# Values multiplied in pairs of key tiles, with three steps of probabilities kept, in an attention and state-space kernel

## The chip, the cores and the metric

The kernel runs on one core of one Trainium2 chip. The metric is the device time of one execution, in microseconds (us); several executions are timed and the median is given. One more execution is recorded by the profiler, and all rows below are of that one.

## The reference, cut to what matters

Two residual blocks follow each other. The first is attention with styles, for a batch of 8, a sequence of 1024, a width of 512 and 16 heads of 32:

```python
x = x + attention(x, cond, ...)     # the block that the change touches
x = x + scan_block(x, cond, ...)    # a gated state-space scan, untouched

# in attention, for every batch and head (x is styled and normalised before)
q, k, v = heads(x @ Wq.T * q_dc), heads(x @ Wk.T * k_dc), heads(x @ Wv.T * v_dc * s2)
attn = softmax(q @ k.T * scale)
out = attn @ v
out = out @ Ww.T * w_dc + skip @ Wu.T * u_dc
```

All inputs, probabilities and values are fp32.

## The kernel before, in words

One program runs two stages in turn: attention, then the scan. Attention works in 32 units, a unit being one batch with a group of 4 heads (`GH`), and in each unit in 16 steps: 2 query chunks of 512 columns (`c`), and in each of them 8 key tiles of 128 keys (`kt`, `TT` = 8). A step `n` has these pieces for its key tile:

- `S`: four score matmuls, one a head, each into a PSUM bank of its own (L802).
- `E`: four exponentials on ScalarE (L948), from the banks into SBUF. For `kt` = 0 they go into `acc` (two chunks deep), for the others into `prob`, which has two slots; step `n` writes slot `n % 2`.
- `C`: the values. Four narrow matmuls, 128 keys by 32 columns of V each, the four heads side by side in the four groups of 32 columns of TensorE's array (L815), added up in one PSUM bank over the 8 key tiles of the chunk. fp32 makes two instructions of each matmul, so the rows show 8 for a piece.
- `A`: for `kt` = 1 to 6, GpSimd adds the four tiles of `prob` to `acc` (L1126), so as to have the sum over keys. The first of them changes `acc`, which `C` of `kt` = 0 reads, so it waits for that `C`.

After a chunk comes `N`: eight narrow matmuls with ones, four over `prob` of `kt` = 7 (L827) and four over `acc` (L831), which give the softmax sums; the latter wait for the last `A`. Then ScalarE copies the sums out (L954), VectorE inverts them (L1074) and multiplies the values (L1084).

Other work, the side work, shares the engines: for the next unit the projections of queries and keys (`pm`, L773) and a pass over all scores to find their maxima (`mx`, L785, reduced by VectorE at L1055), and for the batch the values (L726), the skip path (L744, transposes at L736), the output (L754), the normalisation (L1109 on GpSimd) and the scaling of weights (L1115 on GpSimd).

The order of the instructions on each engine is fixed when the program is built, by a planner (`Order`, L105): each lane is a list of pieces with an assumed cost, what they come after and which bank they take, and the planner always places the piece that can start first by its own clock, and of pieces that can start together the one that is due first. Pieces of one lane and one engine keep their order. The main lane is what `attend` lists (L365 to L408). On TensorE it reads: S(0), S(1), C(0), S(2), C(1), and so on; C(7) and then N come behind the S of the next chunk's first step. `S` takes one of banks 0 to 3, side work takes one of banks 2 to 5, the values lie in bank 6 or 7. Side work may not be placed before its due step. On the chip each engine executes its list in order and waits on semaphores.

The exponential of step `n` writes a slot of `prob` when its last user is done: `C` and `A` of step `n - 2`, or, where step `n - 2` was the last of a chunk (`kt` = 7), `C` and `N` of it (L934 to L947).

Of the kernel before, what the change touches and what calls it, by code (L numbers as in the profile page):

```python
# [16 lines left out]
P = 128  # L17
HID = 512
HEADS = 16
DH = HID // HEADS  # L20
GH = P // DH
# [5 lines left out]
NX = 3 * NST  # L27
EPS_LN = 1e-5
EPS_DEMOD = 1e-8
BANK = 512  # L30
TAPS = 4
UNIT = 8
# [187 lines left out]
    return h, qc * (TT // NQ) + t, qc, kc  # L220


def attention_plan(plan, B, TT, NQ):
    plan.bank = {}
    order = Order(plan, 8, (0.2, 0.2))
# [139 lines left out]
    def attend(u):  # L365
        out, put_ = lane()
        b, g = divmod(u, GROUPS)

        def put(t, *a, **k):
            put_(*a, **k)  # L370
            out[-1]["due"] = u * n_steps + t - 1.0
        for n in range(n_steps + 3):
            if n < n_steps:
                c, kt = divmod(n, TT)

                if kt == 0:
                    v = u * NQ + c - 2
                    old = lambda h: (("N", v // NQ, v % NQ),) if v >= 0 else ()
                else:
                    v = u * n_steps + n - 2  # L380
                    v -= 2 if v % TT == 0 else 0
                    last = ("N", v // n_steps, v % n_steps // TT) if v % TT == TT - 1 else None
                    old = lambda h: (("C", v // n_steps, v % n_steps), last or ("A", v // n_steps, v % n_steps, h)) if v >= 0 else ()
                for h in range(GH):
                    s = ("S", u, n, h)
                    put(n, "PE", 0.24, s, (("mst", u),) if n == 0 else (), [("pe_m{m}", 1)], take=EXP, group=s,
                        step=u * n_steps + n)
                    put(n, "ACT", 0.6, ("E", u, n, h), (s,) + old(h), [("act_m{m}", 1)], group=s, give=True)
            if 0 < n <= n_steps:
                k = n - 1  # L390
                c, kt = divmod(k, TT)
                put(n - 0.5, "PE", 1.0, ("C", u, k), tuple(("E", u, k, h) for h in range(GH)) + (("mv_o", b, TT - 1),),
                    [("pe_av", 1)], take=(6 + (u * NQ + c) % 2,) if kt == 0 else None, group=("av", u, c))
                if 0 < kt < TT - 1:
                    for h in range(GH):
                        put(n - 0.5, "POOL", 1.28, ("A", u, k, h), (("E", u, k, h),) + (
                            (("C", u, k - 1),) if kt == 1 else (("A", u, k - 1, h),)), [("pool_acc", 1)])
            if n and n % TT == 0:
                c = n // TT - 1
                g = ("N", u, c)  # L400
                put(n, "PE", 1.95, g, tuple(("A", u, c * TT + TT - 2, h) for h in range(GH)), [("pe_m{m}", 1)], take=SIDE, group=g)
                put(n, "ACT", 0.6, ("R", u, c), (g,) + ((("D", u - (c == 0), (c - 1) % NQ),) if u or c else ()),
                    [("act_m{m}", 1)], group=g, give=True)
                put(n, "DVE", 3.4, ("I", u, c), (("R", u, c),), [("dve_norm", 1)])
                put(n, "DVE", 0.7, ("D", u, c), (("I", u, c), ("C", u, c * TT + TT - 1)) + (
                    (("f_mm", b - 1, (c + 1) * TT // NQ - 1, HT - 1),) if b else ()), [("dve_norm", 1)], group=("av", u, c), give=True)
        return out
# [34 lines left out]
class Attention:  # L442
    def __init__(self, nc, ctx, d, ident, ones32, B, S):
# [36 lines left out]
        setup.close()  # L480
        self.qhat = sb("qhat", [P, 2, GH, S], F32R)
        self.khat = sb("khat", [P, 2, GH, S], F32R)
        self.prob = sb("prob", [P, 2 * GH, QC])

        self.aoT = sb("aoT", [P, GROUPS, S])

# [218 lines left out]
    def tensor(self, pe):  # L705
# [4 lines left out]
        for p in plan.pieces:  # L710
# [66 lines left out]
            elif kind == "mx":  # L777
                u, j = at
                m = plan.bank[p]
                h, qt, qc, c = score_tile(j, TT, self.NQ)  # L780
                s = u % 2
                for k in (2 * qc, 2 * c + 1):
                    self.half_laid(w, u, k)
                self.empty(w, m, p)
                pe.matmul(bank[m][:, 0:QC], self.qhat[0:96, s, h, qt * P:(qt + 1) * P],  # L785
                          self.khat[0:96, s, h, c * QC:(c + 1) * QC], start=True, stop=True).then_inc(sem[f"pe_m{m}"], 1)
            elif kind == "mt":
                u, = at
                m = plan.bank[p]
                w.wait_ge(sem["dve_mx"], plan.after("dve_mx", ("mxr", u)))  # L790
                self.empty(w, m, p)
                pe.transpose(bank[m][0:GH * TT, 0:P], self.mx[:, :], ident[:, :]).then_inc(sem[f"pe_m{m}"], 1)
            elif kind == "S":
                u, n, h = at
                m = plan.bank[p]
                c, kt, a = self.step(u, n)
                s = u % 2
                w.wait_ge(sem["kones"], 2)
                self.laid(w, u)
                w.wait_ge(sem[f"ld_mrow{s}"], plan.after(f"ld_mrow{s}", ("mst", u)))  # L800
                self.empty(w, m, p)
                pe.matmul(bank[m][:, 0:QC], self.khat[0:98, s, h, kt * P:(kt + 1) * P],  # L802
                          self.qhat[0:98, s, h, c * QC:(c + 1) * QC], start=True, stop=True).then_inc(sem[f"pe_m{m}"], 1)
            elif kind == "C":
                u, n = at
                c, kt, a = self.step(u, n)
                b, g = divmod(u, GROUPS)
                w.wait_ge(sem["dve_v"], plan.after("dve_v", ("mv_o", b, TT - 1)))
                if u * self.NQ + c > 1:

                    w.wait_ge(sem["dve_norm"], plan.after("dve_norm", ("D", *divmod(u * self.NQ + c - 2, self.NQ))))
                for h in range(GH):
                    self.of_bank(w, "act", ("S", u, n, h), ("E", u, n, h))
                    of = self.acc[:, a, h, :] if kt == 0 else self.prob[:, (n % 2) * GH + h, :]
                    mm = pe.matmul(bank[6 + a][h * DH:(h + 1) * DH, 0:QC], self.value(b, kt, g)[:, h * DH:(h + 1) * DH],  # L815
                                   of, start=kt == 0, stop=kt == TT - 1)
                mm.then_inc(sem["pe_av"], 1)
            elif kind == "N":
                u, c = at
                m = plan.bank[p]  # L820
                a = (u * self.NQ + c) % 2
                self.empty(w, m, p)

                n = c * TT + TT - 1
                for h in range(GH):
                    self.of_bank(w, "act", ("S", u, n, h), ("E", u, n, h))
                    pe.matmul(bank[m][h * DH:(h + 1) * DH, 0:QC], self.ones32[:, :], self.prob[:, (n % 2) * GH + h, :],  # L827
                              start=True, stop=False)
                for h in range(GH):
                    w.wait_ge(sem["pool_acc"], plan.after("pool_acc", ("A", u, n - 1, h)))  # L830
                    mm = pe.matmul(bank[m][h * DH:(h + 1) * DH, 0:QC], self.ones32[:, :], self.acc[:, a, h, :],  # L831
                                   start=False, stop=True)
                mm.then_inc(sem[f"pe_m{m}"], 1)
# [22 lines left out]
    def scalar(self, act):  # L856
        sem, plan, w, TT, QC, bank = self.sem, self.plan, Waits(act), self.TT, self.QC, self.bank
        w.wait_ge(sem["x_dve"], 2 * TT + 3)
        for p in plan.pieces:
# [65 lines left out]
            elif kind == "E":  # L925
# [8 lines left out]
                        self.of_bank(w, "pe", old, old)  # L934
                    to = self.acc[:, a, h, :]
                else:
                    v = u * self.NQ * TT + n - 2
                    v -= 2 if v % TT == 0 else 0
                    if v >= 0:
                        old = divmod(v, self.NQ * TT)  # L940
                        w.wait_ge(sem["pe_av"], plan.after("pe_av", ("C", *old)))
                        if v % TT == TT - 1:
                            sums = ("N", old[0], old[1] // TT)
                            self.of_bank(w, "pe", sums, sums)
                        else:
                            w.wait_ge(sem["pool_acc"], plan.after("pool_acc", ("A", *old, h)))
                    to = self.prob[:, (n % 2) * GH + h, :]  # L947
                act.activation(to, bank[m][:, 0:QC], ACT.Exp, scale=SCALE).then_inc(sem[f"act_m{m}"], 1)  # L948
            elif kind == "R":
                u, c = at  # L950
# [145 lines left out]
    def gpsimd(self, pool):  # L1096
# [5 lines left out]
        for p in plan.pieces:  # L1102
# [14 lines left out]
            elif kind == "A":  # L1117
# [1 line left out]
                c, kt, a = self.step(u, n)  # L1119
                self.of_bank(w, "act", ("S", u, n, h), ("E", u, n, h))  # L1120
                if kt == 1:
                    w.wait_ge(sem["pe_av"], plan.after("pe_av", ("C", u, n - 1)))
                    self.of_bank(w, "act", ("S", u, n - 1, h), ("E", u, n - 1, h))
                else:
                    w.wait_ge(sem["pool_acc"], plan.after("pool_acc", ("A", u, n - 1, h)))
                pool.tensor_tensor(self.acc[:, a, h, :], self.acc[:, a, h, :], self.prob[:, (n % 2) * GH + h, :],  # L1126
                                   ALU.add).then_inc(sem["pool_acc"], 1)


# [1245 lines left out]
```

## Time and profile before

| | |
|---|---|
| median of 3 runs | 6185.2 us (6185.17 to 6187.26) |
| profiled execution | 6190.7 us, span 6188.9 us |
| TensorE busy | 5830.7 us, 94% of the span |
| VectorE, ScalarE, GpSimd busy | 72%, 39%, 52% |
| attention | about the first 3150 us of the span |

Busy times are of instructions as the profiler records them; a matmul's recorded time is longer than the distance to the next one, since matmuls are pipelined, so TensorE's busy share says little, and the distances between starts say more. PE is TensorE's matmuls, PEld its weight loads, DVE VectorE, ACT ScalarE, POOL GpSimd.

### The profile page before, as it was taken

How to read it: one execution, taken by the hardware profiler on the slowest of the kernel's cores; microseconds unless marked ns; L12 is line 12 of the kernel's file. 1: busy time of each engine (PE TensorE's matmuls, PEld its weight loads, DVE VectorE, ACT ScalarE, POOL GpSimd, SP SyncE). 2: the span in 40 equal slices, each digit the busy share in tenths (PEclk: the TensorE clock that was granted, in tenths of full speed). 3: DMA queues.
4: the chain of work that ended last, by engine and by line, in shares of the span. 5: the costliest groups of instructions: out<-in, count | busy, mean ns of one | idle time of the engine just before them, and what ended most of it. 6: DMA issues, size and time to landing. Idle time of an engine off the chain costs nothing. (4 is left out here: it accounts for less than half of the span.)

```text
span 6188.9 us, 73250 instructions
## 1 busy us (share of the span) xinstructions
PE 5830.7 (94%) x24000; PEld 2703.2 (44%) x24000; DVE 4474.3 (72%) x5676; ACT 2407.5 (39%) x4698; POOL 3217.6 (52%) x2625
## 2 busy tenths in 40 slices
PE   7999999999999999999986879999999999999998
PEld 3444444444444444444443424444443444444343
DVE  4656656556556566565546998999999898999983
ACT  2444444445444454444453424243332423334111
POOL 1876767677667776775743323425243443524213
PEclk7999999999999999999988889999999999999999
DMA  2332323333232332323213343534444443544433
GB/s 86 89 91 69 99 73 94 91 88 89 76 96 77 98 93 69 106 60 96 82 67 109 87 113 103 147 96 131 110 116 126 121 133 89 150 96 128 115 91 115
DMA packets 411565, 613.30 MB, mean 99 GB/s; under 512 B 58768, under 2 KB 189968, under 8 KB 410672
## 3 DMA queue, kind: packets, MB, share of 16 engines
q1 hardware_dynamic: 374320, 558.24, 32.4%
q10 hardware_dynamic: 36864, 50.38, 3.2%
q8 instruction: 190, 3.11, 0.2%
q14 instruction: 191, 1.56, 0.1%
HBM read 305.31 MB, written 201.38 MB: 82 GB/s over the span
## 5 line engine op out<-in xcount | busy, mean ns | idle before, releaser
L1126 POOL TENSOR_TENSOR acc<-acc,prob 128x512 f32<-128x512 f32 x1536 | 1906.4, 1277 | 837.3 <-PE bank L815 570.8
L1055 DVE TENSOR_REDUCE mx<-bank 128x1 f32<-128x512 f32 x2048 | 1307.4, 684 | 535.9 <-PE bank L785 529.6
L2091 DVE SCALAR_TENSOR_TENSOR g<-xps,bd,g 128x1024 f32<-128x1024 f32 x1024 | 1313.2, 1282 | 143.8 <-PE xps L1806 68.1
L1806 PE MATMUL xps<-sx,spread 128*128 128x512 f32 x2048 | 910.4, 529 | 140.6 <-DVE g L2091 126.0
L948 ACT ACTIVATE prob<-misc 128x512 f32<-128x512 f32 x1277 | 713.5, 599 | 739.0 <-PE misc L802 653.6
L785 PE MATMUL bank<-khat,qhat 96*128 96x512 f32 x2048 | 939.1, 519 | 5.9 <-DVE mx L1055 0.9
L2097 DVE TENSOR_SCALAR g<-g,lim 128x1024 f32<-128x1024 f32 x1024 | 892.7, 872 | 34.8
L1806 PEld LDWEIGHTS xps<-sx,spread 128*128 128x128 f32 x2048 | 359.0, 195 | 693.8 <-issue 368.0
L802 PE MATMUL misc<-qhat,khat 98*128 98x512 f32 x1443 | 602.6, 460 | 17.8 <-ACT prob L948 11.7
L785 PEld LDWEIGHTS bank<-khat,qhat 96*128 96x128 f32 x2048 | 373.8, 192 | 532.5 <-issue 381.4
L1820 PE MATMUL yps<-g,cexp 128*32 128x512 f32 x4096 | 585.4, 630 | 0.1
L773 PE MATMUL bank<-xhT,wqk 128*128 128x512 f32 x1024 | 490.7, 606 | 2.6 <-ACT rsum L954 1.7
L815 PE MATMUL bank<-prob,V 128*32 128x512 f32 x3584 | 489.4, 616 | 0.0
L1763 PE MATMUL miscb<-x2T_sb,w_in 128*128 128x512 f32 x952 | 473.5, 607 | 8.1 <-DMA x2T_sb<-scratch_x2T 8.1
L1860 PE MATMUL miscb<-w_out,ygT 128*128 128x512 f32 x944 | 467.9, 605 | 1.7 <-ACT ygT L2031 1.3
L2231 POOL TENSOR_TENSOR cexp<-cd,mask 128x256 f32<-128x256 f32 x128 | 78.8, 616 | 721.3 <-DVE g L2097 463.0
L1830 PE MATMUL miscb<-w_in,x2T_t 128*128 128x512 f32 x896 | 434.1, 604 | 2.5 <-DMA x2T_t<-scratch_x2T 2.4
L802 PEld LDWEIGHTS misc<-qhat,khat 98*128 98x128 f32 x1443 | 270.6, 190 | 253.4 <-issue 115.0
L2270 POOL TENSOR_TENSOR y_t<-y_t,dx_t 128x512 f32<-128x512 f32 x118 | 150.5, 1276 | 441.9 <-DVE g L2097 333.0
L1046 DVE SCALAR_TENSOR_TENSOR halves<-bank,qk_dc,halves 128x512 fp32r<-128x512 f32 x128 | 95.2, 744 | 372.7 <-ACT halves L912 372.6
L1074 DVE RECIPROCAL rsum<-rsum 128x512 f32<-128x512 f32 x64 | 214.3, 3349 | 190.5 <-ACT rsum L954 190.5
L1910 ACT ACTIVATE xr<-miscb,temb 128x128 f32<-128x128 f32 x476 | 135.6, 368 | 555.5 <-PE miscb L1763 555.5
(221 smaller groups left out, 7189.6 us busy)
## 6 DMA issues: line engine op xcount, KB each, us to landing
sx<-scratch_xhl SPq DMA_DIRECT2D x512, 128.0 KB, 4.9
scratch_dx<-dx SPq DMA_DIRECT2D x64, 512.0 KB, 3.2
scratch_xhl<-xhi SPq DMA_DIRECT2D x64, 512.0 KB, 4.9
scratch_xhl<-xn SPq DMA_DIRECT2D x64, 512.0 KB, 5.1
scratch_y<-ysb SPq DMA_DIRECT2D x512, 64.0 KB
dx_t<-scratch_dx SPq DMA_DIRECT2D x59, 512.0 KB, 6.1
y_t<-scratch_y SPq DMA_DIRECT2D x59, 512.0 KB, 3.9
xt_n<-in_x SPq DMA_DIRECT2D x112, 256.0 KB, 3.0
```

The lines of the kernel that those rows point to most:

```text
L773: mm = pe.matmul(bank[m][:, 0:QC], self.wqk[:, n, it, :], self.xhT[:, it, c * QC:(c + 1) * QC], start=it == 0, stop=it == HT - 1)
L785: pe.matmul(bank[m][:, 0:QC], self.qhat[0:96, s, h, qt * P:(qt + 1) * P], self.khat[0:96, s, h, c * QC:(c + 1) * QC], start=True, stop=Tru ...
L802: pe.matmul(bank[m][:, 0:QC], self.khat[0:98, s, h, kt * P:(kt + 1) * P], self.qhat[0:98, s, h, c * QC:(c + 1) * QC], start=True, stop=Tru ...
L815: mm = pe.matmul(bank[6 + a][h * DH:(h + 1) * DH, 0:QC], self.value(b, kt, g)[:, h * DH:(h + 1) * DH], of, start=kt == 0, stop=kt == TT - 1)
L948: act.activation(to, bank[m][:, 0:QC], ACT.Exp, scale=SCALE).then_inc(sem[f"act_m{m}"], 1)
L1055: dve.tensor_reduce(self.mx2[:, h * TT + qt, c:c + 1], bank[m][:, 0:QC], AX.X, ALU.max).then_inc(sem[f"dve_m{m}"], 1)
L1126: pool.tensor_tensor(self.acc[:, a, h, :], self.acc[:, a, h, :], self.prob[:, (n % 2) * GH + h, :], ALU.add).then_inc(sem["pool_acc"], 1)
L1763: mm = pe.matmul(bank[m][:, :], self.w_in[:, it, ct * P:(ct + 1) * P], self.x2T[:, it, :, :].rearrange("p b q -> p (b q)"), start=it == 0, ...
L1806: mm = pe.matmul(self.xps[t % 2][:, half * BANK:(half + 1) * BANK], self.spread[:, 2 * part + half, :], self.sx[:, n % 2, wd, :], start=Tr ...
L1820: mm = pe.matmul(bank[2 + m][32 * j:32 * (j + 1), :], self.cexp[:, h, tc, :], self.g[:, (t + tp) % 4, half * BANK:(half + 1) * BANK], star ...
L2091: dve.scalar_tensor_tensor(self.g[:, t % 4, :], self.xps[t % 2][:, :], self.bd[:, i % 2, tl:tl + 1], self.g[:, (t - 1) % 4, :], ALU.mult, ...
L2097: dve.tensor_scalar(self.g[:, t % 4, :], self.g[:, t % 4, :], self.lim[:, i % 2, 0, tl:tl + 1], self.lim[:, i % 2, 1, tl:tl + 1], ALU.min, ...
```

## The change

`C` is made once for two key tiles, at each odd `kt`: eight narrow matmuls (16 instructions), first the four of the even tile and then the four of the odd one, each four with a semaphore increment of their own. On TensorE's list it reads: S(0), S(1), S(2), C(0, 1), S(3), S(4), C(2, 3), and so on, with C(6, 7) and N behind the S of the next chunk's first step. The planner is told 1.9 for the piece in place of 1.0 for each half. `prob` has three slots, filled in turn by the steps with `kt` > 0 alone (`ring`), so an exponential waits for the user of three such steps ago; the first `A` of a chunk waits for the first half of C(0, 1). `prob` grows from 16 to 24 KB a partition, and the memory set aside for descriptors of dynamic DMAs falls from 2048 to 512 bytes.

```diff
+PROBS = 3
+def ring(u, n, TT, NQ):
+    c, kt = divmod(n, TT)
+    return ((u * NQ + c) * (TT - 1) + kt - 1)
+def ring_user(r, TT, NQ):
+    c, kt = divmod(r, TT - 1)
+    return c // NQ, c % NQ * TT + kt + 1
...
-                    v = u * n_steps + n - 2
-                    v -= 2 if v % TT == 0 else 0
-                    last = ("N", v // n_steps, v % n_steps // TT) if v % TT == TT - 1 else None
-                    old = lambda h: (("C", v // n_steps, v % n_steps), last or ("A", v // n_steps, v % n_steps, h)) if v >= 0 else ()
+                    r = ring(u, n, TT, NQ) - PROBS
+                    uu, nn = ring_user(r, TT, NQ)
+                    last = ("N", uu, nn // TT) if nn % TT == TT - 1 else None
+                    old = lambda h: (("C", uu, nn | 1), last or ("A", uu, nn, h)) if r >= 0 else ()
...
-                put(n - 0.5, "PE", 1.0, ("C", u, k), tuple(("E", u, k, h) for h in range(GH)) + (("mv_o", b, TT - 1),),
-                    [("pe_av", 1)], take=(6 + (u * NQ + c) % 2,) if kt == 0 else None, group=("av", u, c))
+                if kt % 2:
+                    put(n - 0.5, "PE", 1.9, ("C", u, k), tuple(("E", u, j, h) for j in (k - 1, k) for h in range(GH)) + (
+                        ("mv_o", b, TT - 1),), [("pe_av", 2)], take=(6 + (u * NQ + c) % 2,) if kt == 1 else None,
+                        group=("av", u, c))
                 if 0 < kt < TT - 1:
                     for h in range(GH):
                         put(n - 0.5, "POOL", 1.28, ("A", u, k, h), (("E", u, k, h),) + (
-                            (("C", u, k - 1),) if kt == 1 else (("A", u, k - 1, h),)), [("pool_acc", 1)])
+                            (("C", u, k),) if kt == 1 else (("A", u, k - 1, h),)), [("pool_acc", 1)])
...
-        self.prob = sb("prob", [P, 2 * GH, QC])
+        self.prob = sb("prob", [P, PROBS * GH, QC])
...
-                for h in range(GH):
-                    self.of_bank(w, "act", ("S", u, n, h), ("E", u, n, h))
-                    of = self.acc[:, a, h, :] if kt == 0 else self.prob[:, (n % 2) * GH + h, :]
-                    mm = pe.matmul(bank[6 + a][h * DH:(h + 1) * DH, 0:QC], self.value(b, kt, g)[:, h * DH:(h + 1) * DH],
-                                   of, start=kt == 0, stop=kt == TT - 1)
-                mm.then_inc(sem["pe_av"], 1)
+                for n in (last - 1, last):
+                    kt = n % TT
+                    for h in range(GH):
+                        self.of_bank(w, "act", ("S", u, n, h), ("E", u, n, h))
+                        of = self.acc[:, a, h, :] if kt == 0 else self.prob[:, ring(u, n, TT, self.NQ) % PROBS * GH + h, :]
+                        mm = pe.matmul(bank[6 + a][h * DH:(h + 1) * DH, 0:QC], self.value(b, kt, g)[:, h * DH:(h + 1) * DH],
+                                       of, start=kt == 0, stop=kt == TT - 1)
+                    mm.then_inc(sem["pe_av"], 1)
...
-    nc = bacc.Bacc("TRN2", target_bir_lowering=False, num_devices=1, dynamic_dma_scratch_size=2048)
+    nc = bacc.Bacc("TRN2", target_bir_lowering=False, num_devices=1, dynamic_dma_scratch_size=512)
```

The reads of `prob` in `N` and `A` and the waits of `E` and `A` follow the same new numbering.

## Rows read from the trace of the kernel before

**Rows 1.** The page: busy time and share of each engine

```profile
PE 5830.7 (94%) x24000; PEld 2703.2 (44%) x24000; DVE 4474.3 (72%) x5676; ACT 2407.5 (39%) x4698; POOL 3217.6 (52%) x2625
```

**Rows 2.** Busy time by stretch: start:end, length, busy of each engine, clock, DMA

```profile
1500.00:2000.00 500.00, 486.05 (x2076) 230.57 (x2069) 301.13 (x452) 227.18 (x421) 348.58 (x282) 0.99 0.29 84
3050.00:3100.00 50.00, 43.14 (x183) 15.01 (x184) 11.21 (x15) 25.99 (x49) 40.97 (x34) 0.81 0.30 103
```

**Rows 3.** TensorE's groups by line, from 200 to 3100 us

```profile
L802 PE MATMUL misc<-qhat,khat 98*128 98x512 f32 x1405 | 585.0, 459 | 12.6 <-ACT prob L948 10.1 <-DMA qhat<-mrow 1.6
...
L815 PE MATMUL bank<-prob,V 128*32 128x512 f32 x3472 | 469.4, 612 | 0.0
...
L815 PE MATMUL bank<-acc,V 128*32 128x512 f32 x496 | 66.1, 605 | 0.0
```

**Rows 4.** TensorE in order of time, last unit: start, length, instructions

```profile
3071.17 0.39 PE L802 MATMUL bank<-qhat,khat 98*128 98x512 f32 x1
3071.40 0.39 PE L802 MATMUL misc<-qhat,khat 98*128 98x512 f32 x1
3071.63 0.40 PE L802 MATMUL bank<-qhat,khat 98*128 98x512 f32 x1
3071.96 1.07 PE L815 MATMUL bank<-prob,V 128*32 128x512 f32 x8
3072.95 0.50 PE L802 MATMUL misc<-qhat,khat 98*128 98x512 f32 x1
```

**Rows 5.** TensorE in order of time, narrow pieces back to back

```profile
603.16 2.19 PE L815 MATMUL bank<-prob,V 128*32 128x512 f32 x16
605.28 3.70 PE L773 MATMUL bank<-xhT,wqk 128*128 128x512 f32 x8
...
660.92 1.06 PE L815 MATMUL bank<-prob,V 128*32 128x512 f32 x8
661.80 1.04 PE L827 MATMUL bank<-prob,ones 128*32 128x512 f32 x8
662.66 1.04 PE L831 MATMUL bank<-acc,ones 128*32 128x512 f32 x8
663.63 0.50 PE L785 MATMUL bank<-khat,qhat 96*128 96x512 f32 x1
```

**Rows 6.** What TensorE's matmuls waited for, 200 to 3100 us

```profile
PE bank L792 <- DVE mx L1063: 41.6, 31, 1.9
PE misc L802 <- ACT prob L948: 10.1, 22, 1.2
PE bank L802 <- ACT rsum L954: 9.3, 20, 3.0
```

**Rows 7.** Who waited for the adds of GpSimd (L1126), 200 to 3100 us

```profile
  ACT prob L948: 47.6, 37
  PEld bank L831: 3.3, 4
```

**Rows 8.** GpSimd's groups by line, 200 to 3100 us

```profile
L1126 POOL TENSOR_TENSOR acc<-acc,prob 128x512 f32<-128x512 f32 x1488 | 1847.0, 1277 | 729.3 <-PE bank L815 566.9 <-ACT prob L948 127.3 <-issue 35.1
L1109 POOL TENSOR_TENSOR xt_n<-xt_n,brow 128x512 f32<-128x512 f32 x109 | 139.0, 1278 | 83.8 <-DMA xt_n<-in_x 82.9 <-ACT prob L948 0.7
L1115 POOL TENSOR_TENSOR wwu<-wwu,brow 128x512 f32<-128x512 f32 x62 | 79.7, 1285 | 31.9 <-DMA wwu<-in_wwT 31.9
```

**Rows 9.** GpSimd in order of time, at the ends of chunks

```profile
654.48 3.77 POOL L1126 TENSOR_TENSOR acc<-acc,prob 128x512 f32<-128x512 f32 x3
...
669.46 9.95 POOL L1126 TENSOR_TENSOR acc<-acc,prob 128x512 f32<-128x512 f32 x8 [5.88 <-PE bank L815]
...
884.81 5.00 POOL L1126 TENSOR_TENSOR acc<-acc,prob 128x512 f32<-128x512 f32 x4
906.21 4.96 POOL L1126 TENSOR_TENSOR acc<-acc,prob 128x512 f32<-128x512 f32 x4 [16.40 <-PE bank L815]
...
3104.53 6.24 POOL L1126 TENSOR_TENSOR acc<-acc,prob 128x512 f32<-128x512 f32 x5 [3.90 <-PE bank L815]
```

**Rows 10.** TensorE in order of time, the sums that wait for them

```profile
897.20 1.04 PE L831 MATMUL bank<-acc,ones 128*32 128x512 f32 x8
...
904.97 1.06 PE L815 MATMUL bank<-acc,V 128*32 128x512 f32 x8
```

**Rows 11.** The page: VectorE's maxima, the group by line

```profile
L1055 DVE TENSOR_REDUCE mx<-bank 128x1 f32<-128x512 f32 x2048 | 1307.4, 684 | 535.9 <-PE bank L785 529.6
```

**Rows 12.** The page: DMA issues, with the queue that issues them

```profile
sx<-scratch_xhl SPq DMA_DIRECT2D x512, 128.0 KB, 4.9
scratch_dx<-dx SPq DMA_DIRECT2D x64, 512.0 KB, 3.2
...
xt_n<-in_x SPq DMA_DIRECT2D x112, 256.0 KB, 3.0
```

More of the change, by code:

```diff
@@ L804, in tensor @@
             elif kind == "C":
-                u, n = at
-                c, kt, a = self.step(u, n)
+                u, last = at
+                c, _, a = self.step(u, last)
                 b, g = divmod(u, GROUPS)
@@ L826, in tensor @@
                     self.of_bank(w, "act", ("S", u, n, h), ("E", u, n, h))
-                    pe.matmul(bank[m][h * DH:(h + 1) * DH, 0:QC], self.ones32[:, :], self.prob[:, (n % 2) * GH + h, :],
+                    pe.matmul(bank[m][h * DH:(h + 1) * DH, 0:QC], self.ones32[:, :], self.prob[:, ring(u, n, TT, self.NQ) % PROBS * GH + h, :],
                               start=True, stop=False)
@@ L936, in scalar @@
                 else:
[L937 to L942, printed above, removed]
+                    r = ring(u, n, TT, self.NQ) - PROBS
+                    if r >= 0:
+                        old = ring_user(r, TT, self.NQ)
+                        w.wait_ge(sem["pe_av"], plan.after("pe_av", ("C", old[0], old[1] | 1)) - (1 - old[1] % 2))
+                        if old[1] % TT == TT - 1:
                             sums = ("N", old[0], old[1] // TT)
@@ L946, in scalar @@
                             w.wait_ge(sem["pool_acc"], plan.after("pool_acc", ("A", *old, h)))
-                    to = self.prob[:, (n % 2) * GH + h, :]
+                    to = self.prob[:, ring(u, n, TT, self.NQ) % PROBS * GH + h, :]
                 act.activation(to, bank[m][:, 0:QC], ACT.Exp, scale=SCALE).then_inc(sem[f"act_m{m}"], 1)
@@ L1121, in gpsimd @@
                 if kt == 1:
-                    w.wait_ge(sem["pe_av"], plan.after("pe_av", ("C", u, n - 1)))
+                    w.wait_ge(sem["pe_av"], plan.after("pe_av", ("C", u, n)) - 1)
                     self.of_bank(w, "act", ("S", u, n - 1, h), ("E", u, n - 1, h))
@@ L1125, in gpsimd @@
                     w.wait_ge(sem["pool_acc"], plan.after("pool_acc", ("A", u, n - 1, h)))
-                pool.tensor_tensor(self.acc[:, a, h, :], self.acc[:, a, h, :], self.prob[:, (n % 2) * GH + h, :],
+                pool.tensor_tensor(self.acc[:, a, h, :], self.acc[:, a, h, :], self.prob[:, ring(u, n, TT, self.NQ) % PROBS * GH + h, :],
                                    ALU.add).then_inc(sem["pool_acc"], 1)
```

## The prediction, made before the changed kernel was run

> **What bounds the kernel now.** I read the page first: TensorE is busy 94% of the span, the next engine 72% [rows 1]. The stretches come next, since the change touches attention alone, roughly the first 3150 of 6189 us. In the middle of it, from 1500 to 2000 us, TensorE is busy 486 of 500 us at a clock of 0.99, which is the level of 2.4 GHz, VectorE 301, ScalarE 227 and GpSimd 349 [rows 2]. The waits say the same: of 2900 us TensorE's matmuls waited 42 us for the maxima at the unit's end and some 20 us for banks that ScalarE had to empty [rows 6]. So attention goes by what TensorE has to execute, in a fixed order, and a piece made cheaper there is worth its own size, unless a new wait takes it back.
>
> The candidate for such a wait is GpSimd. The reader should see three numbers. A chunk lasts 2900 us / (496 / 8) = 46.8 us, since 496 rows are the eight instructions of C(0) of each chunk [rows 3], so a step lasts 5.85 us. The 24 adds of a chunk take 24 x 1.277 = 30.7 us, and with the 171 side pieces, 3.5 us a chunk, GpSimd is busy for 34 of 46.8 us [rows 8]. The adds run back to back from kt = 1 on, and the idle time lies in front of the first of them, which waits for C(0): 567 us in all [rows 8].
>
> **What a piece of C costs.** The order in time of the last unit shows it free of other work: scores start 0.23 us apart (3071.17, 3071.40, 3071.63), the piece of C starts 0.33 us behind the last score, and the next score 0.99 us behind the piece [rows 4]. Where narrow pieces stand together, the distances are 0.88, 0.86 and then 0.97 us [rows 5]. Eight more narrow instructions cost 0.86 to 0.88 us, then, and what is left of a lone piece is the price of going from wide to narrow (0.33 - 0.23 = 0.10 us) and back (0.99 - 0.86 = 0.13 us): 0.23 us.
>
> **What is removed.** 32 units of 16 steps have 512 pieces of C; the stretch of 2900 us holds (3472 + 496) / 8 = 496 of them [rows 3]. Half of them, 256, join another and lose 0.23 us each: 59 us. Two pieces of C already stand together in 8 places of the stretch, like the one of 603.16 [rows 5], where nothing is to be saved on that score, so I take 57 us. C(7) next to N stays what it was. The number of instructions, their data and the semaphore increments are the same.
>
> The bound from the other side is the row at 603.16: two pieces in 2.12 us [rows 5], which is 2.12 + 0.10 = 2.22 us against 2 x 1.09 = 2.18 us for two lone ones, no saving at all. Something inside that pair waited; the second piece needs exponentials of its own step, which had just been scored. In the changed order four scores of the next step stand between a step's last score and its C, nearly everywhere, and the even half of the pair is a whole step old, so I go by the clean rows: 0.23 us; the range keeps nothing as the other end.
>
> For the same switch the Trainium skill ("TensorEngine Tiling (Array Packing)", Key Properties) says that a change of tiling mode drains the engine; it gives no figure. The page "TensorE: Matmul & The Clock Gate" (Part 3, Measured speedup vs the span model) counts a pack as one matmul and some 4 ns for each further tile, without a term for the switch; by that alone the estimate would be 4 x 4 ns a pair, and the sum 0 to 5 us. The rows' 0.23 us speaks against leaving the switch out.
>
> **What is added: the first add of a chunk starts later.** A(1) waits for C(0), which now stands behind S(2) and not behind S(1). At least the four scores of S(2), 4 x 0.23 = 0.9 us, come in between; at most a whole step, 5.85 us. Behind that GpSimd's 24 adds shift as a whole, and N (its second half, L831) must not find them unfinished. Now it rarely does: it waited in 4 cases, 3.3 us in all [rows 7]. How near it is: the adds end at 658.25 and L831 starts at 662.66, 4.4 us later; in another chunk they end at 889.81 and L831 starts at 897.20, 7.4 us later [rows 5, 9, 10]. The first add of the next chunk then starts at 669.46 and 906.21 [rows 9], the latter 1.2 us behind the start of C(0) at 904.97 [rows 10]. I take a shift of about 3 us, since side work gets in between but the scores of a late lane are due first; it fits into 4 to 7 us of slack in most chunks. For chunks with much side work on GpSimd I charge 5 us in all.
>
> **The third slot.** An exponential waits for the adds of three steps ago. Now ScalarE waits 48 us in 37 cases for adds [rows 7]. The first that binds is E(4) for A(1), where it was E(3) for A(1): A(1) starts up to a step later, and its user comes a step later, so the slack there is the same and grows afterwards. TensorE hardly feels these waits (10 us of them reach it, [rows 6]). I count 0, bounded by 0 and -48 us. For its C the exponential need not wait: each such piece stands before the S that the exponential needs anyway. With two slots the pair would have been different: E(3) overwrites what C(0, 1) reads.
>
> **The last unit** has no side work. There GpSimd sets the pace (41 of 50 us busy, and TensorE's granted clock is 0.81 on the mean, between its levels of 2.4 and 1.2 GHz [rows 2]), and between two chunks it idles 3.90 us until C(0) [rows 9]. There the shift costs its full 0.9 us for S(2) and somewhat more where the clock is low; for two chunks I charge 3 us.
>
> **Edits that cost nothing.** The longer `prob` moves SBUF addresses; the smaller descriptor memory would matter for DMAs issued by GpSimd, and the page's issue rows name the queue of SyncE, with that of ScalarE for a few, and never GpSimd's [rows 12]. The piece is one lump of 1.85 us in which TensorE fills no other bank: VectorE can be short of maxima to reduce for at most 0.5 us a pair (1.85 us less two side banks at 0.68 us each [rows 11]), which its idle time of 199 in 500 us covers [rows 2]. The scan stage isn't touched.
>
> **Sum.** Profiled execution 6190.7 - 57 + 5 + 3 = 6142 us; the median lies 5.5 us below the profiled execution, so 6136 us, 0.8% faster.
>
> **Rivals.**
>
> *The sums become late (slower).* If A(1) shifts by nearly a whole step, 5.85 us, the slack of 4.4 to 7.4 us is used up in half of the chunks, and since N blocks the main lane on TensorE, the next chunk starts late, with its A(1) later in turn. It decides the sign once the mean lateness exceeds 57 / 64 = 0.9 us a chunk. With a shift of 5.85 us against a slack of 4.4 us each chunk loses 1.5 us, in all 93 us: 6185 + 93 - 57 + 3 = 6224 us. For it: the adds run without a gap behind A(1). Against it: GpSimd idles 12.7 us of a chunk, and the planner knows of the dependence and puts other pieces first. Chance 0.13.
>
> *The switch saves nothing, or is paid back as waits for banks (same).* Either the pair costs 2.12 us as at 603.16, or TensorE, 57 us ahead, waits for ScalarE and VectorE to empty banks, or the late sums and the saving cancel. Time 6185 us. For it: the row at 603.16. Against it: TensorE's waits for banks are some 20 us in 2900 now [rows 6]. The skill's page on tiling (PSUM Bottleneck) warns of this: packed matmuls run faster, emptying PSUM doesn't. Here VectorE's and ScalarE's shares speak against it. Chance 0.14.
>
> *The third slot gives more (faster still).* If the 48 us of ScalarE's waits for adds were holding up the scores and vanish, 6136 - 48 = 6088 us. For it: 37 waits of 1.3 us; with a slot more the scores can run a step ahead of GpSimd. Against it: only 10 us of waits on the exponentials show on TensorE [rows 6]. Chance 0.15.
>
> *The forecast:* 6136 us, with 6115 to 6165 us for it alone (0.58).
>
> **Chances and range.** Faster by over 0.2% (below 6173 us; less than 0.2% a measurement of this kernel can hardly tell from none): the forecast, the third slot, and a small share of the rest: 0.75. Within 0.2%: 0.13. Slower: 0.12. The range, 6080 to 6195 us, takes in the whole of the third slot's gain and the case of no gain, and leaves out most of the late sums.
>
> **What would show it.** After the change the rows of L815 should come as x16, 1.85 us from the start to the next wide matmul, and some 256 fewer switches; scores and maxima unchanged in number and distance. The wait of the first add for L815 moves from C(0) to the pair, and GpSimd's idle time before it grows by about 3 us a chunk, with the waits of L831 for the adds under 20 us in all. ScalarE's wait for adds should fall. The scan stage should last as long as before. The prediction is wrong if L831 waits for adds in most chunks, if the pair takes over 2 us, or if the planner, with pieces of 1.9 in place of 1.0, spreads the side work so that TensorE idles at the ends of units more than now.

## The result, and the profile after

The changed kernel is slower: 6212.0 us median (6204.7 to 6224.7, 5 runs) against 6186.0 us (6185.2 to 6191.1, 5 runs), a ratio of 1.0041 (95% interval 1.0026 to 1.0056). 6136 us was forecast, with a chance of 0.12 for slower. All runs of both are of the same, undisturbed state. Ratios to the kernel before, run beside each time, are given from here on, since chips differ: its medians beside the experiments went from 6188 to 6206 us.

The page of the changed kernel, busy time and share of each engine, to be held against [rows 1]:

```profile
span 6204.6 us, 73243 instructions
...
PE 5809.4 (94%) x24000; PEld 2731.6 (44%) x24000; DVE 4472.1 (72%) x5676; ACT 2406.0 (39%) x4698; POOL 3216.1 (52%) x2625
```

TensorE is busy 21 us less and the span is 16 us longer, with the same 24000 matmuls. The first instruction of the scan's recurrence (the group of L2091 before, L2107 after) starts at 3323.5 us before and at 3339.2 us after, and from there to its last one it is 2773 us in both: all of the loss lies ahead of it.

Two stretches, for [rows 2]:

```profile
1500.00:2000.00 500.00, 481.97 (x2090) 237.82 (x2089) 301.63 (x453) 232.28 (x430) 352.43 (x285) 0.99 0.30 85
3050.00:3100.00 50.00, 45.34 (x200) 20.13 (x199) 20.41 (x29) 25.79 (x49) 39.66 (x33) 0.90 0.34 114
```

In the middle TensorE is idle 18 us of 500 where it was 14. Now TensorE in order of time, for [rows 4, 5]: first a pair with scores around it.

```profile
3083.20 1.06 PE L832 MATMUL bank<-acc,V 128*32 128x512 f32 x8
3084.09 1.04 PE L832 MATMUL bank<-prob,V 128*32 128x512 f32 x8
3085.06 0.50 PE L817 MATMUL misc<-qhat,khat 98*128 98x512 f32 x1
3085.40 0.62 PE L817 MATMUL bank<-qhat,khat 98*128 98x512 f32 x2
```

Then, earlier, a pair with the sums behind it.

```profile
661.81 1.92 PE L832 MATMUL bank<-prob,V 128*32 128x512 f32 x16
663.55 1.04 PE L844 MATMUL bank<-prob,ones 128*32 128x512 f32 x8
664.41 1.04 PE L848 MATMUL bank<-acc,ones 128*32 128x512 f32 x8
665.38 0.50 PE L800 MATMUL bank<-khat,qhat 96*128 96x512 f32 x1
```

A pair lasts 3085.06 - 3083.20 = 1.86 us, as forecast. The rows also show what I overlooked: the first wide matmul behind narrow ones has 0.34 us to the next one (3085.06 to 3085.40), where scores are 0.23 us apart. So leaving a narrow stretch costs 0.11 us more, and a switch there and back 0.10 + 0.13 + 0.11 = 0.34 us. The 0.11 us doesn't belong to narrow matmuls alone: such a matmul is recorded with 0.50 us in place of 0.40, and others like it stand behind transposes (0.32 us to the next one) and, as shown further down, where a score or maxima matmul had to wait (0.34 us).

What the matmuls waited for, 200 to 3100 us, for [rows 6]:

```profile
PE bank L807 <- DVE mx L1079: 55.9, 31, 2.5
PE misc L817 <- ACT prob L964: 11.9, 49, 0.7
PE bank L817 <- ACT rsum L970: 11.9, 21, 3.4
PE bank L759 <- DVE mx L1071: 6.3, 1, 6.3
PE bank L788 <- DVE halves L1062: 4.4, 7, 0.6
PE bank L848 <- POOL acc L1142: 4.0, 4, 3.5
```

The wait for the maxima at the unit's end grew from 41.6 to 55.9 us, there are small new ones, and the sums wait 4 us for the last add. These rows count only time in which no matmul is recorded as running, and show but a part. The distances between starts show all of it. I summed them over units 1 to 31 (from the first score of the first unit to that of the last), took 0.23 us for a matmul of scores or maxima, 0.43 us for one of the two instructions of a wide fp32 matmul, 0.108 us for one of a transpose or a narrow matmul, and 0.34 us for a switch. The time at 1.2 GHz comes from the trace's record of the granted clock, and half of it counts as lost. What is left are waits, the 0.1 us or so that the matmul behind each wait or transpose loses included.

| us, units 1 to 31 | whole | work | switches | clock | waits |
|---|---|---|---|---|---|
| before | 2919 | 2561 | 525: 179 | 14 | 165 |
| changed | 2931 | 2561 | 280: 95 | 35 | 240 |
| difference | +12 | 0 | -83 | +20 | +75 |

The switches went as forecast in number and gave more than forecast. The waits took back 75 of the 83 us, and the clock, granted at 1.2 GHz for 55 us (14 falls) between 200 and 3055 us where it was 17 us (5 falls; the table's stretch begins some 50 us earlier), put the kernel behind. The last unit and the start of the scan add another 4 us.

GpSimd's adds, for [rows 7 to 9]: first who waited for them from 200 to 3100 us (us, times), then the end of a chunk and the next chunk's first add in order of time.

```profile
  ACT prob L964: 42.9, 26
  PEld bank L848: 8.2, 6
```

```profile
657.41 5.04 POOL L1142 TENSOR_TENSOR acc<-acc,prob 128x512 f32<-128x512 f32 x4
664.06 2.52 POOL L1131 TENSOR_TENSOR wwu<-wwu,brow 128x512 f32<-128x512 f32 x2 [1.62 <-DMA wwu<-in_wwT]
673.99 14.89 POOL L1142 TENSOR_TENSOR acc<-acc,prob 128x512 f32<-128x512 f32 x12 [7.41 <-PE bank L832]
```

In the mean of 60 chunks (units 2 to 31) the first add starts 15.0 us behind the chunk's first score, where it was 9.6: a shift of 5.4 us. The time from the last add to the sums over `acc` fell from 5.3 to 3.1 us. Here it is 664.41 - 662.45 = 2.0 us. GpSimd's idle time in front of the adds didn't grow as expected (729 us before [rows 8], 669 us now, 200 to 3100 us); that in front of its side pieces did, from 116 to 191 us.

### The profile page after: what moved, and what is told of

Its sections match the earlier page's. It is cut to its first block and busy times, and to the rows that moved or that the text cites. A ratio compares the mean times of both kernels' runs of the same rounds, so it can differ in the third digit from the quotient of the medians.

```text
span 6204.6 us, 73243 instructions
## 1 busy us (share of the span) xinstructions
PE 5809.4 (94%) x24000; PEld 2731.6 (44%) x24000; DVE 4472.1 (72%) x5676; ACT 2406.0 (39%) x4698; POOL 3216.1 (52%) x2625
## 5 line engine op out<-in xcount | busy, mean ns | idle before, releaser
L2107 DVE SCALAR_TENSOR_TENSOR g<-xps,bd,g 128x1024 f32<-128x1024 f32 x1024 | 1312.8, 1282 | 148.0 <-PE xps L1822 71.7
L964 ACT ACTIVATE prob<-misc 128x512 f32<-128x512 f32 x1336 | 748.6, 598 | 633.4 <-PE misc L817 524.2
L817 PE MATMUL misc<-qhat,khat 98*128 98x512 f32 x1503 | 645.1, 465 | 19.8 <-ACT prob L964 13.6
L832 PE MATMUL bank<-prob,V 128*32 128x512 f32 x3584 | 455.5, 616 | 0.5 <-ACT prob L964 0.3
```

What stands on the lines that cost most here:

```text
L2107: dve.scalar_tensor_tensor(self.g[:, t % 4, :], self.xps[t % 2][:, :], self.bd[:, i % 2, tl:tl + 1], self.g[:, (t - 1) % 4, :], ALU.mult, ...
```

## The experiments

Two theories stood at first: the late add (the first add of a chunk starts later, and the sums and the next chunk with it), and the lump (two pieces of C in one bring waits of TensorE by themselves, or by the order that the planner makes around them).

**ring3_single** is the changed kernel with C once a step, cost 1.0, so that only the third slot is left of the change.

> The third slot alone, with C once a step as before. Late-add theory (the pair delays the first add of a chunk, and with it the sums and the next chunk) and order theory (the planner's new order for lumps of 1.9 brings more waits for banks and at unit ends): both expect no difference, 6180 to 6190 us. A theory that the third slot itself costs or gives something: outside that.

Measured: 1.0001 (0.9991 to 1.0010). The third slot gives and costs nothing beyond 0.1%. This kernel serves as the base below.

**late_add** takes ring3_single and changes the wait of the first add alone, in the planner and on the chip:

```diff
-                            (("C", u, last_of(k - 1, TT)),) if kt == 1 else ...      # last_of(k - 1, TT) is k - 1 here
+                            (("C", u, k),) if kt == 1 else ...
...
-                    w.wait_ge(sem["pe_av"], plan.after("pe_av", ("C", u, last_of(n - 1, TT))) - ...)
+                    w.wait_ge(sem["pe_av"], plan.after("pe_av", ("C", u, n)))
```

> Three slots, C once a step as before, but the first add of a chunk waits for C of key tile 1 in place of C of key tile 0, in the planner and on the chip. Late-add theory: the first adds start some 4 to 5 us later, the slack before the sums shrinks, and the time rises by 40 to 80 us over the third slot alone, to 6225 to 6265 us. Order theory: 6180 to 6195 us, since no lump is made.

Measured: 1.0085 (1.0070 to 1.0100), some 52 us. Over units 1 to 31 its waits are 34 us and its lost clock 14 us above ring3_single's. So a late first add is dear where nothing is saved for it. The waits don't appear on the sums but as a late chunk: who waited for the adds in late_add from 200 to 3050 us (L856 are the sums), and then what the matmuls waited for (L825 are the scores, L796 the projections).

```profile
  PEld bank L856: 15.3, 17
  ACT prob L972: 9.8, 9
  PE bank L856: 4.8, 2
```

```profile
PE bank L825 <- ACT rsum L978: 28.9, 16, 3.0
...
PE bank L796 <- ACT rsum L978: 10.4, 6, 1.7
```

Scores and projections wait 39 us in all until ScalarE has copied the sums out of their bank; in ring3_single these two rows are 11.6 and 1.7 us.

**shift_pairs** and **first_alone** pair other key tiles, so that C of key tile 0 stands alone and the first add isn't late.

For each key tile, `LASTS` has the one with which its C is made:

```diff
-LASTS = (0, 1, 2, 3, 4, 5, 6, 7)     # ring3_single
+LASTS = (0, 2, 2, 4, 4, 6, 6, 7)     # shift_pairs: 0, (1,2), (3,4), (5,6), 7
+LASTS = (0, 1, 3, 3, 5, 5, 7, 7)     # first_alone: 0, 1, (2,3), (4,5), (6,7)
```

> Pairs of key tiles (1,2), (3,4), (5,6), with 0 and 7 alone: three quarters of the switches saved (192 x 0.23 = 44 us), and the first add waits for C(0) behind S(1) as before. Late-add theory: 6135 to 6155 us. Order theory: the lumps are still there, 6185 to 6215 us.

> Key tiles 0 and 1 alone, pairs (2,3), (4,5), (6,7) as in the change: 44 us of switches saved, first add as early as before. Late-add theory: 6135 to 6155 us. Order theory: 6185 to 6210 us.

Measured: 1.0054 (1.0039 to 1.0069) and 1.0038 (1.0023 to 1.0052). The late add is gone and the loss is not: the late-add theory falls as the whole explanation. (6186 x 1.0054 = 6219 us is slower than the order theory expected, too.) first_alone saves 178 switches, 60 us, and has 52 us more waits and 34 us more lost clock than ring3_single.

**single_few_adds** and **pair_few_adds** leave out the adds of key tiles 5 and 6, so the softmax sums lack them (one of the lines; the waits for the last add change with it).

```diff
-                if 0 < kt < TT - 1:
+                if 0 < kt < 5:
```

> The partner of the next run: C once a step, three slots, and the adds of key tiles 5 and 6 left out (16 adds a chunk in place of 24; the softmax sums lack these two tiles). GpSimd then has 10 us less to do a chunk. Both theories: not much faster than before, since TensorE bounds, 6150 to 6185 us.

> The changed kernel with the same adds left out, so that the sums can't be late for a chunk whose first add starts 5 us later. Late-add theory: 45 to 60 us faster than single_few_adds, the full price of the switches. Order theory (lumps of 1.85 us by themselves bring waits): at most 25 us faster than single_few_adds, or slower.

Measured: 0.9919 (0.9901 to 0.9937) and 0.9969 (0.9957 to 0.9982). GpSimd's adds do hold the kernel back, 8 in 1000 for a third of them, which is more than was expected; but with these out of the way the pair's median is still 27 us behind its partner's, where the late-add theory wanted it 45 to 60 us ahead. So the lump costs by itself, or by the order that the planner makes for it.

**pair_told_22** and **single_told_11** change the planner's cost alone, to 2.2 for a pair and to 1.1 for a single piece.

> The changed kernel, with the planner told 2.2 for a pair in place of 1.9. If the loss is a matter of the order that the planner happens to find (order luck), this moves the time by 15 us or more either way against 6212 us. If the loss is structural (late add, lumps), it stays within 6200 to 6225 us.

> The kernel with C once a step and three slots, with the planner told 1.1 for a C in place of 1.0: the spread that another order gives with nothing changed in the work. Order luck: 15 us or more away from 6190 us. Structural: 6180 to 6200 us.

Measured: 1.0020 (1.0011 to 1.0030) and 0.9970 (0.9956 to 0.9983). Another order moves either kernel by 2 to 3 in 1000 on its side of the gap and doesn't close it.

**before_told_11** and **single_told_12** follow that up.

> The kernel before, two slots, with nothing changed but that the planner is told 1.1 for C in place of 1.0 (0.99 us and 0.10 us for the switch into narrow, by the rows). If the gain of single_told_11 comes from the truer cost: 15 to 20 us faster than before. If the third slot is needed for it: within 5 us of before.

> C once a step, three slots, told 1.2. True-cost theory: slower than told 1.1, as 1.2 is too much. Order luck: anywhere within 20 us of before.

Measured: 0.9991 (0.9981 to 1.0000) and 1.0000 (0.9991 to 1.0010). 1.1 with two slots gives hardly anything, and 1.2 with three nothing. So the gain of single_told_11 doesn't come from a truer cost alone; whether it is a lucky order or needs the third slot beside the cost of 1.1, these runs leave open.

**light_max_single** and **light_max_pair** take each maximum over half of the columns, told 0.42 for 0.69, so that VectorE empties a bank sooner.

```diff
-                dve.tensor_reduce(..., bank[m][:, 0:QC], AX.X, ALU.max)...
+                dve.tensor_reduce(..., bank[m][:, 0:QC // 2], AX.X, ALU.max)...
```

> C once a step, three slots, and the maxima taken over half of each bank's columns (the other 256 are left out), so that VectorE empties a bank in some 0.4 us in place of 0.68 us; the planner is told 0.42. Partner of the next run. Bank theory (scores for the maxima wait for VectorE to empty one of the side banks): faster than before, 6100 to 6160 us on the chip of the first runs.

> The changed kernel with the same lighter maxima. VectorE theory (the lumps bring waits because VectorE runs dry in them and is short of time afterwards): at least 30 us faster than light_max_single, since the switches are saved and VectorE has time to spare. If the waits come from ScalarE's side or from the order of the main lane: still slower than light_max_single, by 10 to 40 us.

Measured: 0.9932 (0.9917 to 0.9947) and 1.0004 (0.9995 to 1.0014). The gap grew to 44 us, against the VectorE theory; but the planner had made new orders for both, and 32 us of the gap are lost clock.

**joined_mix** therefore keeps an order: that of ring3_single is made first, and then only C of key tiles 2, 4 and 6 is moved down to stand right before C of 3, 5 and 7. **joined_pairs** moves C of key tile 0 down to that of 1 as well.

```diff
+    log, later, out = plan.log, {}, []     # plan.log: every piece in the planner's order
+    for piece, signals in log:
+        if to(piece) != piece:             # a C that moves: to(piece) is the one it joins
+            later.setdefault(to(piece), []).append((piece, signals))
+        else:
+            out += later.pop(piece, []) + [(piece, signals)]
```

> The order that the planner makes for single pieces (ring3_single), in which afterwards only C of key tiles 2, 4 and 6 is moved down to stand right before C of 3, 5 and 7; everything else keeps its place. No add becomes late. If the planner's new order was the loss: 192 switches at some 0.34 us saved, ratio to before 0.988 to 0.992. If the lump itself brings the waits (banks run full or dry around it): ratio 0.998 to 1.005.

> The same with C of key tile 0 moved to C of key tile 1 too, so that the first add of a chunk is late without the planner knowing it. Late-add theory: 20 us or more slower than joined_mix although it saves 64 more switches. Without such an effect: 20 us faster than joined_mix.

Measured: 1.0055 (1.0038 to 1.0071) and 1.0114 (1.0099 to 1.0129). So the planner's order isn't the cause: with all else in place, joining three pairs a chunk costs 34 us. Over units 1 to 31 joined_mix has 61 us less of switches than ring3_single, 19 us more lost clock and 83 us more waits. That an exponential might wait for the later C before it may write its slot is no part of this: in neither trace does ScalarE wait for a C. Joining the fourth pair, which makes the first add late, costs 38 us more, though 21 us of switches are saved with it.

What the weight loads waited for shows where the waits are, 200 to 3050 us. First ring3_single (L808 loads for the maxima, L825 for the scores, L815 for the transpose of the maxima at the unit's end):

```profile
PEld misc L825 <- ACT prob L972: 87.0, 224, 2.1
PEld bank L808 <- DVE mx L1079: 81.5, 265, 0.8
PEld bank L815 <- DVE mx L1087: 63.1, 30, 2.8
```

then joined_mix, with L836, L853 and L843 for them:

```profile
PEld bank L836 <- DVE mx L1107: 101.9, 345, 0.5
PEld misc L853 <- ACT prob L1000: 99.2, 227, 3.2
PEld bank L843 <- DVE mx L1115: 71.1, 30, 3.3
```

All three grew, that for VectorE's banks in number most. The distances say the same. Counting each matmul whose record ends over 0.05 us later than the one before it and its own work explain, the switches left out, matmuls of the maxima are held up in 294 cases instead of 115 and for 73 us instead of 28, scores for 94 us instead of 79, and the transpose at the unit's end (by the starts) for 59 us instead of 43: 76 of the 83 us.

One part of ScalarE's lateness has a name in the trace. ScalarE also issues the DMAs that lay out queries and keys (L598), six at a time:

```profile
1215.66 0.60 ACT L1000 ACTIVATE prob<-misc 128x512 f32<-128x512 f32 x1
1215.72 3.78 ACTq L598 DMA_DIRECT2D khat<-halves  x6
1219.62 1.09 ACT L1000 ACTIVATE prob<-misc 128x512 f32<-128x512 f32 x2 [3.36 <-issue]
```

For 3.8 us it empties no bank. In ring3_single one exponential had to wait for that alone (5.6 us, `issue` in the rows), in joined_mix ten (37.3 us), in the changed kernel seven (21.5 us). What these issues cost TensorE, no run tested.

**short_max_single** and **short_max_joined** are ring3_single and joined_mix in their own orders, with the reduction of light_max on the chip and the planner told nothing of it.

> ring3_single in its own order, with the maxima taken over half of each bank's columns (256 left out), the planner still told 0.69. Partner of the next run. Expected 20 to 50 us faster than before, since the matmuls of the maxima wait less: ratio 0.992 to 0.997.

> joined_mix in its own order with the same shorter reduction. If VectorE's time for a bank is what the lump costs: as fast as short_max_single or up to 40 us faster (with the full reduction it was 34 us slower). If the waits for ScalarE or the main lane's own delays are the cost: 20 us or more slower than short_max_single.

Measured: 0.9957 (0.9940 to 0.9974) and 1.0006 (0.9996 to 1.0015), 34 us apart by their medians, as before. The wait of the maxima's matmuls fell to 9 and 35 us, but the waits together are still 72 us above the partner's (scores 103 for 80 us, the transpose 59 for 43 us), and the clock took another 26 us. Of short_max_joined, the weight loads again:

```profile
PEld misc L853 <- ACT prob L1000: 120.4, 259, 3.2
PEld bank L843 <- DVE mx L1115: 70.1, 30, 3.3
PEld bank L836 <- ACT prob L1000: 43.6, 113, 0.9
```

Where VectorE is faster, ScalarE is what TensorE waits for: VectorE's time for a bank isn't the cause by itself.

**sums_joined** joins where a lump stands already: in the order of single_told_11 the last C of a chunk is moved down to stand right before the sums.

> The order for single pieces told 1.1, in which only the last C of a chunk is moved down to stand right before the sums N, so that it stands next to narrow matmuls; some 30 of 64 chunks lose a switch. Expected by the rows: 30 x 0.34 = 10 us faster than single_told_11, ratio to before 0.995 to 0.998. If any joining brings waits: no faster than single_told_11.

Measured: 0.9956 (0.9940 to 0.9972), 6166.3 us beside 6195.0 us of the kernel before. It is the fastest kernel of the study that computes all of the reference, and the only joining that didn't lose. Against single_told_11 its switches fell by 18 (some 30 were expected), its waits by 16 us. Whether it beats that kernel (0.9970, 0.9956 to 0.9983) the intervals leave open.

## Why the prediction was wrong

**The switches: right in number, too small in size.** 523 narrow stretches became 278 between 200 and 3100 us, and a pair lasts 1.86 us. The term was 57 us at 0.23 us a switch; with the 0.11 us that the first wide matmul behind them loses, it is 83 us (245 x 0.34).

**The cover under "Edits that cost nothing": the step that failed.** I costed the lump at nothing, since VectorE idles 199 of 500 us. It cost 75 us of waits in the changed kernel, the late add's share included, and 83 us in joined_mix, where no add is late. The argument was one from a share of busy time, and it asked the wrong question. What counted was what TensorE does between two lumps. Before, C stood once in each step and let ScalarE and VectorE empty banks; with C bunched, scores and maxima follow each other for twice as long. The stretch around 1435 us of the changed kernel shows it:

```profile
1433.82 0.49 PE L800 MATMUL bank<-khat,qhat 96*128 96x512 f32 x1
1434.15 0.39 PE L817 MATMUL misc<-qhat,khat 98*128 98x512 f32 x1
1434.42 0.50 PE L800 MATMUL bank<-khat,qhat 96*128 96x512 f32 x1
1434.76 0.41 PE L817 MATMUL misc<-qhat,khat 98*128 98x512 f32 x1
1435.02 0.50 PE L800 MATMUL bank<-khat,qhat 96*128 96x512 f32 x1
```

A maxima matmul and a score start every 0.60 us (1433.82, 1434.42, 1435.02), where the two by themselves take 0.46 us, and no idle time is reported, because each matmul is recorded with 0.4 to 0.5 us. The other engines' rows over the same time name the pace:

```profile
1433.09 3.07 DVE L1071 TENSOR_REDUCE mx<-bank 128x1 f32<-128x512 f32 x5
1433.32 3.07 ACT L964 ACTIVATE prob<-misc 128x512 f32<-128x512 f32 x5
1434.42 0.19 PEld L800 LDWEIGHTS bank<-khat,qhat 96*128 96x128 f32 x1 [0.27 <-DVE mx L1071]
```

VectorE and ScalarE both work without a gap, 0.61 us a bank each, so once its free banks are used up TensorE can fill a pair of them no faster. The weights of the maxima matmul wait for VectorE and are loaded only at 1434.42, when the matmul itself starts; of the 0.14 us that the pair of matmuls loses, 0.03 us are the wait and 0.11 us the longer distance behind a matmul that waited. It also says why relieving VectorE alone moved the waits: ScalarE's pace is the same. The kernel before has this distance too (maxima matmuls at 1428.64 and 1429.24), but there a C ends it after two of them. That joining costs is shown (joined_mix); that the missing pause between scores is the reason is my reading of where the waits appeared. It is the rival "paid back as waits for banks", which I took to end at no change and gave 0.14, on the ground that TensorE's own idle rows show only 20 us of such waits. That ground was weak: by the starts the kernel before had 165 us of waits over 2919 us. The warning of the Trainium skill ("TensorEngine Tiling (Array Packing)", PSUM Bottleneck) that emptying PSUM does not speed up with packed matmuls pointed the right way: the waits grew by 75 us. One of the prediction's own signs of being wrong came true as well, more idle time of TensorE at the ends of units (41.6 to 55.9 us).

**The late add: mis-sized.** A shift of about 3 us was forecast and 5.4 us measured. The waits of the sums stayed small, 12 us as the prediction said they would. The cost doesn't appear there but in the chunk behind. Alone it is 52 us (late_add), over joined_mix 38 us with 21 us of switches saved; I charged 5 us. In the changed kernel itself its share is smaller: first_alone has no late add and 69 switches more (23 us), and both have nearly the same ratio, so I estimate some 25 us for the late add together with what joining the fourth pair costs. The rival "the sums become late" was right in sign and near in time (6224 us), but as the main cause it is refuted.

**The third slot: right** at 0 us; the rival that it gives 48 us is refuted. ScalarE's wait for adds hardly fell (47.6 to 42.9 us).

**The clock wasn't in the sum.** It cost 20 us more in the changed kernel, and 14 to 38 us more than in ring3_single or the partner in all others with pairs or a late add, but for sums_joined (3 us).

The falls go with the waits. All 5 falls of the kernel before came at or within 5 us behind a recorded idle time of TensorE of 1.2 to 3.0 us, and so did 14 of the 15 in joined_mix (1.2 to 2.9 us, ten of them at a unit's end). Of the 14 in the changed kernel 8 came so (2.0 to 6.3 us, six at a unit's end), 5 behind scores that started in twos with 0.2 us of idle time between, and 1 behind neither. So much of the lost clock looks like a second price of the waits, but no run separated the two. Open also is how the 75 us of waits divide between ScalarE's banks, VectorE's and the unit's end: relieving VectorE moved them and lowered the difference to the partner only from 83 to 72 us. ScalarE wasn't relieved in any run.

## What to carry to other kernels

Where an engine executes a fixed order, short pieces of work that wait for nothing are also the pauses in which others empty its buffers; before bunching them, count what stands between two of them afterwards, and hold it against the pace of those that empty (here 0.61 us a bank against 0.46 us for a pair of matmuls that fills one of each). Judge waits of pipelined matmuls by the distances of their starts against the work's own distances, not by idle rows. And when a change joins work and makes a dependence later at once, test the two apart first: here the joining saved 83 us of switches, its waits were of the same size, and the late add alone was worth 52 us.

## What the runs showed of the hardware that I had not expected

- A change between wide and 32-column matmuls costs 0.34 us there and back: 0.10 us in, 0.13 us out, and 0.11 us more on the first wide matmul behind. The Trainium skill ("TensorEngine Tiling (Array Packing)", Key Properties) says that changing the tiling mode drains the engine; the first two figures agree with it.
- A wait costs TensorE some 0.11 us beyond itself: between scores and maxima of the kernel before, from 200 to 3050 us, the 178 matmuls recorded with some 0.50 us, as those are that had to wait, have at least 0.31 us to the next one, most of them 0.34 us or more; the 1578 recorded with some 0.40 us have 0.23 us in the median.
- TensorE's granted clock fell to 1.2 GHz in the midst of attention, from 200 to 3055 us: 5 times and for 17 us before, 14 times and for 55 us after, mostly at or shortly behind idle times of 1.2 to 6.3 us.
- The runs of the changed kernel spread over 20 us (6204.7 to 6224.7), those of before beside them over 6 us; but 14 runs of before on another chip spread over 20 us as well (6183.3 to 6203.0). The longest run has the lowest granted clock (0.966 at 6224.7 us, 0.968 and 0.969 at 6204.7 and 6206.4 us).
